# Splitting w1 of all experts once, into DRAM, in a float32 macaron kernel on one core

## The reference

```
x = x + 0.5 * ffn(layernorm(x))
x = x + attn(layernorm(x))
x = x + 0.5 * ffn(layernorm(x))
```

```
probs = softmax(mean(h, tokens) @ gate_w); top_w, top_i = top_k(probs, 2); top_w /= sum(top_w)
y_e = gelu(h @ w1[e] + b1[e]) @ w2[e] + b2[e];  out = sum over the two of top_w[e] * y_e
```

## Time and profile before

| what | value |
|---|---|
| median of three runs | 274.96 us |
| the profiled execution, its own time | 275.18 us |
| its span | 273.4 us |
| TensorE (PE) busy | 255.6 us (93%) |
| VectorE (DVE) busy | 222.6 us (81%) |
| ScalarE (ACT) busy | 207.2 us (76%) |
| GpSimd (POOL) busy | 45.6 us (17%) |
| granted TensorE clock, mean | 0.997 of full |
| read from HBM, written | 11.85 MB, 2.10 MB |

### The profile page before, as it was taken

How to read it: one execution, slowest core, us unless ns; L and a number is a source line. 1 busy time by engine, 2 the same in 40 slices (tenths; PEclk the granted TensorE clock), 3 DMA queues, 4 the chain that set the end, 5 groups by cost and what they waited for, 6 DMA issues and landing times.

```text
span 273.4 us, 3572 instructions
## 1 busy us (share of the span) xinstructions
PE 255.6 (93%) x1056; PEld 177.2 (65%) x1056; DVE 222.6 (81%) x567; ACT 207.2 (76%) x254; POOL 45.6 (17%) x58
## 2 busy tenths in 40 slices
PE   0899999999999989999999999997999999999994
PEld 0796676665656656666566566564777778778781
DVE  3569578559999999999999999999999997546252
ACT  1069584558998959969889979889996697689462
POOL 5320200430006002533006151003000030000000
PEclk9999999999999999999999999999999999999998
DMA  7364310022000022000400005000000500820005
GB/s 208 140 174 135 103 54 0 0 74 84 1 0 0 2 73 82 1 2 0 151 5 0 2 2 154 0 0 2 0 0 2 157 0 0 224 86 0 0 0 153
DMA packets 13762, 14.17 MB, mean 52 GB/s; under 512 B 1008, under 2 KB 9456, under 8 KB 13744
## 3 DMA queue, kind: packets, MB, share of 16 engines
q1 hardware_dynamic: 12720, 12.37, 15.3%
q0 software_dynamic: 352, 1.31, 1.2%
q10 hardware_dynamic: 672, 0.27, 0.4%
HBM read 11.85 MB, written 2.10 MB: 51 GB/s over the span
## 4 chain that ended last, share of the span: by engine, by line
PE 72%; ACT 8%; DVE 8%; issue 7%; DMA 3%; SPq 1%; POOL 0%; ACTq 0%; DVEq 0%; POOLq 0%
PE y_ps L684 32%; PE hid_ps L655 25%; PE aux_ps L752 3%; PE aux_ps L708 3%; PE aux_ps L784 3%; PE aux_ps L733 2%; PE aux_ps L773 2%; ACT vb L558 2%; PE y_ps L792 1%; DMA xt<-x_dram 1%; DVE hid_lo L931 1%; ACT dt_t L547 1%; DMA w_sb<-wpack_dram 1%; ACT hid L475 1%; ACT yt L504 1%
## 5 line engine op out<-in xcount | busy, mean ns | idle before, releaser
L475 ACT ACTIVATE hid<-hid_ps,w_sb 128x1024 f32<-128x1024 f32 x64 | 70.2, 1108 | 19.9 <-PE hid_ps L655 19.6
L684 PE MATMUL y_ps<-hid,w_sb 128*128 128x512 f32 x168 | 79.2, 594 | 0.0
L655 PE MATMUL hid_ps<-z_hi,w_hi 128*128 128x512 f32 x128 | 51.6, 484 | 0.8 <-ACT hid L475 0.8
L684 PEld LDWEIGHTS y_ps<-hid,w_sb 128*128 128x128 f32 x168 | 30.8, 190 | 22.9 <-issue 20.3
L931 DVE TENSOR_TENSOR hid_lo<-hid,hid_hi 128x1024 fp32r<-128x1024 f32 x22 | 26.6, 1222 | 19.8 <-ACT hid_hi L482 19.8
L655 PE MATMUL hid_ps<-z_lo,w_hi 128*128 128x512 f32 x128 | 39.9, 393 | 0.0
L655 PE MATMUL hid_ps<-z_hi,w_lo 128*128 128x512 f32 x128 | 39.8, 392 | 0.0
L655 PEld LDWEIGHTS hid_ps<-z_hi,w_hi 128*128 128x128 f32 x128 | 23.1, 189 | 16.1 <-issue 12.4
L655 PEld LDWEIGHTS hid_ps<-z_hi,w_lo 128*128 128x128 f32 x128 | 24.0, 188 | 5.5
L655 PEld LDWEIGHTS hid_ps<-z_lo,w_hi 128*128 128x128 f32 x128 | 24.0, 188 | 5.5
L482 ACT ACTIVATE hid_hi<-hid 128x1024 fp32r<-128x1024 f32 x22 | 22.7, 1055 | 1.5 <-PE y_ps L684 1.4
(11 more groups left out here) (119 smaller groups left out, 438.7 us busy)
## 6 DMA issues: line engine op xcount, KB each, us to landing
w_sb<-wpack_dram SPq DMA_DIRECT2D x16, 256.5 KB, 3.5
w_sb<-wpack_dram SPq DMA_DIRECT2D x15, 258.0 KB, 3.0
xt<-x_dram SPq DMA_DIRECT2D x3, 512.0 KB, 7.1
out_dram<-xt SPq DMA_DIRECT2D x3, 512.0 KB, 5.8
rope_sb<-rope_dram POOLq DMA_DIRECT2D x1, 1024.0 KB, 7.9
out_dram<-xt SPq DMA_DIRECT2D x2, 256.0 KB, 2.4
xt<-x_dram ACTq DMA_DIRECT2D x1, 256.0 KB, 4.0
xt<-x_dram SPq DMA_DIRECT2D x1, 256.0 KB, 3.6
```

The lines of the kernel that those rows point to most:

```text
L475: nc.scalar.activation(hid[:, slot % HBUF, :], hid_ps[:, slot % 2, :], ACT.Gelu, bias=bias).then_inc(hid_ready, 1)
L655: last = nc.tensor.matmul(hid_ps[:, slot % 2, cols], w, z[:, q % 2, cols], start=first, stop=end)
L684: last = nc.tensor.matmul(y_ps[:, cols], wt, src[:, cols], start=t == 0 and i == 0, stop=t == SLOTS - 1 and end)
```

## The change

What it does:

- w1 of all 8 experts is loaded once into SBUF (w1_all, 2 MB, in two transfers: the first 256 hidden units of every expert before x of batch 1, the rest behind the first expert loads). It uses the space of the mixer's state, gated, va and vb, which are written only when w1_all has been read. ScalarE and VectorE split each expert (c_pre_hi, c_pre_lo at places 206 to 550), four buffers shared with dt_t, decay, alpha and u; SyncE writes high and low parts to an internal DRAM tensor w1_split (8 times 512 KB).
- Passes 2 to 7 load w1's two parts from w1_split (512 KB per expert), ready for up; L465 and L884 are gone for them. Pass 0 splits its two experts' blocks from w1_all (the first two blocks) and from two transfers of its own; pass 1 splits from w1_all. Pass 2's load waits for all eight writes.
- b1 moves from the transfer of w1 to that of w2; a gelu at f = 0 now waits for w2_in[k].
- w2 of the first expert is left unscaled, that of the second is scaled by ratio = coef1 / coef0 (a reciprocal and a multiply on VectorE per pass), and pass_out scales y by coef0.
- The three small operations of mixer_carry_decay go to GpSimd (mixer_carry_steps, places 741, 1166, 1347, 1766). dstep's first value of each chunk is set once to -1000, so that its exponential is 0, in place of the memset of alpha in every mixer.
- The opening: x of batch 0 comes in four quarters; the tiles are turned first, copied out in two halves with their sums, and these sums give the logits; the ones products before the first tile are 13, those behind the logits 5. in_chunk is made earlier on GpSimd; rope is loaded by SyncE, behind x(3), instead of GpSimd.
- PARTS is 3, 0, 0, 0, 0, 3, 4, 4. All places are new. The up and gelu of slot s stand at 40 s + 40, a down at 40 s + 98 or, by parts, 40 s + 132, which is 40 later each. On TensorE m_dt stands at 649, 949, 1309, 1706 and m_v at 669, 989, 1349, 1746; on VectorE f_route at 309, 545, 937, 1258, 1504, 1847, 2189 for passes 1 to 7, m_cos first at 709.

The diff, cut to its core:

```diff
-DOWN = {False: 58, True: 92}
-
-PARTS = {0: 2, 1: 0, 2: 0, 3: 0, 4: 0, 5: 3, 6: 3, 7: 3}
+DOWN = {False: 98, True: 132}
+
+PARTS = {0: 3, 1: 0, 2: 0, 3: 0, 4: 0, 5: 3, 6: 4, 7: 4}
...
+        "f_norm": {1: 166, 2: 306, 3: 749, 4: 1089, 5: 1449, 6: 1806, 7: 2126},
+        "f_route": {1: 229, 2: 449, 3: 926, 4: 1249, 5: 1489, 6: 1829, 7: 2166},
...
+        "c_split_rest": {0: 75, 1: 201},
+        "c_proj": {0: 151},
+        "c_pre_lo": {0: 232, 1: 385, 2: 391, 3: 463, 4: 470, 5: 517, 6: 523, 7: 550},
+        "c_mixer": {0: 487},
+        "f_stats": {1: 81, 2: 207, 3: 400, 4: 959, 5: 1312, 6: 1712, 7: 2053},
...
+        "c_split_rest": {0: 19, 1: 130},
+        "c_pre_hi": {0: 206, 1: 226, 2: 233, 3: 384, 4: 392, 5: 450, 6: 460, 7: 500},
+        "c_proj_hi": {0: 220},
...
+        "m_rms": {0: 459, 1: 773, 2: 1113, 3: 1477},
+        "m_carry": {0: 741, 1: 1166, 2: 1347, 3: 1766},
...
+        "c_pre_out": {0: 238, 1: 392, 2: 397, 3: 472, 4: 479, 5: 525, 6: 532, 7: 560},
+        "f_load": {1: 315, 2: 567, 3: 939, 4: 1262, 5: 1510, 6: 1856, 7: 2195},
...
-    B1_AT, W2_AT, B2_AT = F, F + FT, 2 * F + FT
+    B1_AT, W2_AT, B2_AT = 0, FT, FT + F
+    PRE_BUF = 4
     HBUF = 4
-    WARM = 14
+    WARM_EARLY, WARM = 13, 5
+    HEADS = 2
...
+        late = sb("late", [P, 4, N])
+        state, gated, va, vb = (late[:, i, :] for i in range(4))
+        w1_all = late[:, :, :].rearrange("p a n -> p (a n)").rearrange("p (e n) -> p e n", e=E)
+        w_sb = sb("w_sb", [P, 2, TOP, PACK - F])
...
+        w1_parts = sb("w1_parts", [P, 2, TOP, 2, F], F32R)
+        w1_hi, w1_lo = w1_parts[:, :, :, 0, :], w1_parts[:, :, :, 1, :]
+        w1_split = nc.dram_tensor("w1_split", [E, P, 2 * F], F32, kind="Internal").ap()
...
-                src = []
                 for k in range(TOP):
                     e = sp.value_load(top_i[0:1, k:k + 1], min_val=0, max_val=E - 1)
-                    src.append(wpack[bass.ds(e, 1), :, :].rearrange("e p n -> p (e n)"))
-                    head = P if q == 0 and k == 0 else 0
-                    if head:
-                        sp.dma_start(w_sb[:, 0, 0, 0:head], src[k][:, 0:head]).then_inc(w1_head_in, 16)
-                    sp.dma_start(w_sb[:, q % 2, k, head:W2_AT], src[k][:, head:W2_AT]).then_inc(w1_in[q % 2][k], 16)
-                for k in range(TOP):
-                    sp.dma_start(w_sb[:, q % 2, k, W2_AT:], src[k][:, W2_AT:]).then_inc(w2_in[q % 2], 16)
+                    if q >= 2:
+                        if q == 2 and k == 0:
+                            for i in range(PRE_BUF):
+                                sp.wait_ge(pre_out[i], 16 * (E // PRE_BUF))
+                        sp.dma_start(w1_parts[:, q % 2, k, :, :].rearrange("p a n -> p (a n)").bitcast(F32),
+                                     w1_split[bass.ds(e, 1), :, :].rearrange("e p n -> p (e n)")).then_inc(w1_in[q % 2][k], 16)
+                    if q == 0:
+                        sp.dma_start(w1_first[:, k, :], wpack[bass.ds(e, 1), :, HEADS * P:F].rearrange("e p n -> p (e n)")
+                                     ).then_inc(w1_first_in[k], 16)
+                    sp.dma_start(w_sb[:, q % 2, k, :],
+                                 wpack[bass.ds(e, 1), :, F:].rearrange("e p n -> p (e n)")).then_inc(w2_in[q % 2][k], 16)
+
+            def keep_split(e):
+
+                sp.wait_ge(pre_hi, e + 1)
+                sp.wait_ge(pre_lo, e + 1)
+                sp.dma_start(w1_split[e], mix_tmp[:, e % PRE_BUF, :]).then_inc(pre_out[e % PRE_BUF], 16)
...
-            sp.dma_start(xt[:, 0, 0:NT // 2, :], x0[:, 0:NT // 2, :]).then_inc(x_in[0], 16)
+            for i in range(2):
+                sp.dma_start(xt[:, 0, 2 * i:2 * i + 2, :], x0[:, 2 * i:2 * i + 2, :]).then_inc(x0_in[i], 16)
             sp.dma_start(gate_sb[:, :], gate_w).then_inc(small_in, 16)
+            sp.dma_start(w1_all[:, :, 0:HEADS * P], wpack[:, :, 0:HEADS * P].rearrange("e p n -> p e n")).then_inc(w1_heads_in, 16)
             load_x(1)
             load_experts(0)
+            sp.dma_start(w1_all[:, :, HEADS * P:], wpack[:, :, HEADS * P:F].rearrange("e p n -> p e n")).then_inc(w1_tails_in, 16)
             load_x(2)
             load_x(3)
+            sp.dma_start(rope_sb[:, :, :], rope.rearrange("k p n -> p k n")).then_inc(rope_in, 16)
...
+            def mixer_carry_steps(b):
+
+                pool.wait_ge(cumd_done, b + 1)
+                if b:
+                    pool.wait_ge(small_exp, b)
+                nc.gpsimd.tensor_scalar(small[:, 0, :], first_of(decay), -1.0, None, ALU.mult).then_inc(first_done, 1)
+                nc.gpsimd.tensor_scalar(ncd[:, :], cumd[:, :], cumd[:, 0:1], DECAY_MAX,
+                                        ALU.subtract, ALU.min).then_inc(ncd_done, 1)
+                pool.wait_ge(ncd_done, b + 1)
+                nc.gpsimd.tensor_tensor(small[:, 1, 1:NCH], ncd[:, 0:NCH - 1], ncd[:, 1:NCH],
+                                        ALU.subtract).then_inc(small_done, 1)
...
+            chosen = []
+
+            def split_first():
+
+                act.wait_ge(w1_heads_in, 16)
+                act.wait_ge(index_ready, 1)
+                chosen.extend(act.value_load(top_i[0:1, k:k + 1], min_val=0, max_val=E - 1) for k in range(TOP))
+                for f in range(HEADS):
+                    rows = slice(f * P, (f + 1) * P)
+                    nc.scalar.activation(w1_hi[:, 0, 0, rows],
+                                         w1_all[:, bass.ds(chosen[0], 1), rows].rearrange("p e n -> p (e n)"),
+                                         ACT.Copy).then_inc(w1_head_hi, 1)
+            def split_rest(k):
+
+                if k:
+                    nc.scalar.activation(w1_hi[:, 0, k, 0:HEADS * P],
+                                         w1_all[:, bass.ds(chosen[k], 1), 0:HEADS * P].rearrange("p e n -> p (e n)"),
+                                         ACT.Copy).then_inc(w1_hi_ready, 1)
+                act.wait_ge(w1_first_in[k], 16)
+                nc.scalar.activation(w1_hi[:, 0, k, HEADS * P:], w1_first[:, k, :], ACT.Copy).then_inc(w1_hi_ready, 1)
+
+            def split_second(q):
+
+                act.wait_ge(w1_tails_in, 16)
+                act.wait_ge(index_ready, q + 1)
                 for k in range(TOP):
-                    head = P if q == 0 and k == 0 else 0
-                    if head:
-                        act.wait_ge(w1_head_in, 16)
-                        nc.scalar.activation(w1_hi[:, 0, 0, 0:head], w_sb[:, 0, 0, 0:head],
-                                             ACT.Copy).then_inc(w1_head_hi, 1)
-                    act.wait_ge(w1_in[q % 2][k], 16 * (q // 2 + 1))
-                    nc.scalar.activation(w1_hi[:, q % 2, k, head:], w_sb[:, q % 2, k, head:F],
+                    e = act.value_load(top_i[0:1, k:k + 1], min_val=0, max_val=E - 1)
+                    nc.scalar.activation(w1_hi[:, q, k, :], w1_all[:, bass.ds(e, 1), :].rearrange("p e n -> p (e n)"),
                                          ACT.Copy).then_inc(w1_hi_ready, 1)
+
+            def presplit_hi(e):
+
+                act.wait_ge(w1_tails_in, 16)
+                if e >= PRE_BUF:
+                    act.wait_ge(pre_out[e % PRE_BUF], 16 * (e // PRE_BUF))
+                nc.scalar.activation(mix_tmp[:, e % PRE_BUF, 0:F].bitcast(F32R), w1_all[:, e, :],
+                                     ACT.Copy).then_inc(pre_hi, 1)
...
+                if f == 0:
+                    act.wait_ge(w2_in[q % 2][k], 16 * (q // 2 + 1))
...
-                                         bias=bias2[:, q % 2, :]).then_inc(yt_ready, 1)
+                                         bias=bias2[:, q % 2, :], scale=coef[:, q % 2, 0:1]).then_inc(yt_ready, 1)
...
+            turn_z(0)
             read_logits(0)
-            turn_z(0)
+            split_first()
             top_tanh(0)
-            split_w1(0)
...
-                for slot in slot_at(tick, 0):
+                for slot in slot_at(tick, TICKS):
...
+            for _ in range(WARM_EARLY):
+                nc.tensor.matmul(hid_ps[:, 0, 0:P], ones[:, :], ones[:, :], start=True, stop=True)
+            pe.wait_ge(made_ident, 2)
+            pre_norm(0)
...
+            def presplit_lo(e):
+
+                dve.wait_ge(pre_hi, e + 1)
+                V.tensor_tensor(mix_tmp[:, e % PRE_BUF, F:].bitcast(F32R), w1_all[:, e, :],
+                                mix_tmp[:, e % PRE_BUF, 0:F], ALU.subtract).then_inc(pre_lo, 1)
...
+                V.reciprocal(inverse[:, :], coef[:, q % 2, 0:1]).then_inc(inverse_ready, 1)
+                dve.wait_ge(inverse_ready, q + 1)
+                V.tensor_tensor(ratio[:, q % 2, :], coef[:, q % 2, 1:2], inverse[:, :], ALU.mult).then_inc(ratio_ready, 1)
...
-                V.tensor_scalar(small[:, 0, :], first_of(decay), -1.0, None, ALU.mult).then_inc(first_done, 1)
+                    dve.wait_ge(small_done, b)
                 V.tensor_tensor_scan(cumd[:, :], last_of(decay), cum_cap[:, :], 0.0,
```

(8 more changed lines are left out.)

384 lines of the change are left out of this document (227 added, 157 removed), and 6 rows, old and new, of the table AT.

## The result

The changed kernel takes 268.97 us (median of 4 runs, 268.60 to 269.13) against 275.12 for the kernel before on the same chip: a ratio of 0.9777, 95% interval 0.9757 to 0.9798, so 6.1 us less. The forecast was 269.8. The profiled execution took 268.60 us with a span of 266.8, against 275.18 and 273.4: 6.6 us less span. The experiments ran beside runs of the kernel before whose median was 275.1 to 275.6, so they are compared by ratio; 0.001 is 0.28 us.

The account below looks back on a forecast made before the run. TensorE was taken to bound the kernel, with VectorE also full beside the mixers. Parts 2.0 less, last slot 0.5 more, waits 2.2 less and opening 1.5 less make 5.2 us less: 269.8 us, range 266.0 to 274.4.

Parts of the forecast that it names:

- Parts, 2.0 less: Passes 0, 6, 7: 28 instead of 22 slots by parts, each 1.40 instead of 1.72 us, 2.0 us less TensorE work.
- The last slot, 0.5 back: Tail: by parts, the last slot's first half is complete later, so yt overlaps less; 0.5 us more, between 0 and 0.86.
- Waits, 2.2 less: Middle stretch with the mixers: VectorE relieved by about 8 us, so TensorE's 5.15 us of waits shrink by 2.2.
- Rival 1: Middle stretch: VectorE's relief is worth nothing, the 5.15 us of waits are ScalarE's; 272.0 us, chance 0.16.
- Opening, 1.5 less: Opening: earlier index, first up and gelu; up 4 done at about 28.5 us, 1.5 us less, ends 0 and 3.4.
- last tile 9.97: Opening: the last normalised tile ends at 9.97 us, from which the index follows at about 12.95, 0.3 earlier.
- Transfers at nothing: Passes 2 to 7: the 512 KB loads of w1 parts, taken as 4.5 us, all fit their covers; cost nothing.
- Rival 4: Mixers: carry steps held on GpSimd make ScalarE wait 16 us, half reaching TensorE; 277.8 us, chance 0.09.

Follow-up runs that it names:

- the order by halves: The changed kernel with the last slot's six matmuls ordered half by half, all three terms of half 0, then of half 1: 269.25 us, ratio 0.9776.
- the last run: The changed kernel with 9 warming products behind the logits and slot 63, the very last, back in plain float32: 268.44 us, ratio 0.9748.

## Why the prediction was right, and where not

The forecast was 5.2 us less against the profiled execution, and its span is 6.6 less. That the median came within 0.8 us of the forecast is in part luck: the opening and the waits gave 2.4 us more than the sum had, the parts and the tail 1.0 less.

**Parts, 2.0 less: 1.2 measured** by TensorE's busy time, though six times 1.72 less 1.40 is work that it doesn't do; taken back, they are worth 2.3. The time of ScalarE and VectorE for it was costed at nothing because both had time to spare in those stretches. In the changed kernel that held: TensorE is idle 0.01 us from 20.20 to 66 us and 0.04 from 215 on. But the reason given doesn't carry it, since put alone into the kernel before, where there is as much to spare, the slots cost 6 us, most of it behind one hid_lo. Spare time of an engine over a stretch is not slack of each slot, nor of what stands behind it, and the prediction never priced that.

**The last slot, 0.5 back: 0.7 measured, the mechanism right.** The overlap of yt with the last matmuls fell from 0.74 to 0.11 us, which is the 0.6 that the prediction had before it took a little off for issue gaps; 0.1 more comes behind yt's start. The last hid_lo is just in time: the last two matmuls' weights wait 0.18 us for it, but the matmuls start 0.46 us behind the two before them (260.34 and 259.88), as those did. What it does is to keep the order by halves from helping, and the prediction didn't look at when it is there. That this slot should stay plain is shown by the last run.

**Waits, 2.2 less: 2.9 measured** by TensorE's idle time, 2.1 if the 0.8 us by which TensorE's busy time came out long is put here. The reason given was VectorE's relief. For the same work of TensorE in the mixers VectorE does some 7 us less (144.53 us beside 141.85 of TensorE before, 142.48 beside 146.80 now), where the sum had 8; an estimate. The runs with dummy work show that in the new order VectorE's load reaches the end at one half and ScalarE's at a fifth; that relief without the new places would have given the same is not shown. Rival 1 (worth nothing) would have left the 5.15 us of waits; 2.24 are left. VectorE was forecast under 140 us in 147; it is 142.48 in 149, 140.6 of 147: just missed. The sum took less than half of the waits because some were ScalarE's; over half went.

**Opening, 1.5 less: 3.2 measured, the one term well off.** The end of up 4 was put at 28.5 and came at 26.94. Of these 1.6 us, 1.0 is the index: predicted out at 12.95, out at 11.94. The step "last tile 9.97" kept the time of the earlier trace rows, but the last tile is done at 9.14. The first statistics begin at 3.35 in place of 4.37, x coming in quarters, and VectorE's last four tiles start at 8.02 and take 1.12 us in place of 8.45 and 1.52; beside the latter GpSimd filled in_chunk (0.95 us from 8.37), which the change makes earlier. Whether that is what stretched them was not tried. A further 0.2 is w2's transfer (gelu 1.2 earlier in all, at 16.21 where 17.4 was said), and 0.4 the walk from gelu 0 to the end of up 4, 11.1 us said and 10.73 measured. The upper end of this term, 3.4, had the result in it. The mechanism, first blocks without a transfer, is borne out by the run that undoes it: 3.2 us back, of which some 1.5 are the transfer. The rest of the gain is the earlier index (1.3 us) and a gelu that no longer stands behind the rounding of the second expert's w1.

**Transfers at nothing: right.** With another 512 KB in front of each the w1 parts still come in time, and w2 of pass 7 no longer does. The write to DRAM took 2.8 us where 5.8 had been taken.

**Rival 4: its mechanism came, its price did not.** The GpSimd steps were held in mixer 3, by 3.4 us together, but where ScalarE had other work: 0.7 us of waiting there, none on TensorE. The Trainium skill (SBUF — State Buffer, SBUF: two separate sides) says that a VectorE operation with two SBUF inputs holds the shared port pair for its whole length and a GpSimd operation that reads SBUF then blocks; the trace agrees, as each held step ends within 0.2 us of the end of such a tensor_tensor. That it costs little here is a matter of places, and the run with the steps on VectorE is slower.

## What to carry to other kernels

Before more work is given to an engine that has time to spare over a stretch, price the slack of one unit of it, from the instruction that makes its input to the one that waits for its output, and look at what stands behind it in that engine's order: a routing step behind an instruction that waits is late with all that hangs on it. Where a middle stretch is full on two engines, try how much of a dummy operation reaches the end, for each engine alone; that gives the exchange rate for edits that add such work to this order. Where a run undoes one thing, read in its chain of waits that the edit moved nothing else. And the last unit of a kernel is to be chosen for how early its first half is complete, not for its total cost.

## What the runs showed of the hardware

- Around the 1.45 us without work ahead of the first up, TensorE's granted clock falls to 0.50 for some 6 us in some executions of the same kernel and stays at 1.00 in others; with four more small products there it fell in none of 15 executions (mean 0.993 to 0.998). The Trainium skill (TensorE: Matmul & The Clock Gate, Part 1: The HAM clock gate) says that the half rate is the default and activity releases it, and that when it is released varies from run to run with the same kernel; here the fall does, at 0.984 and 0.996 mean clock of one kernel.
- 512 KB written to DRAM out of SBUF landed 2.8 us after issue (8 writes), 512 KB read from there 4.3 (12 reads); 128 KB asked for right behind the index landed after 2.0.
- ScalarE took 1.4 to 1.5 us to read two indexes out of SBUF into its registers: from 11.94 to 13.44 us in the changed kernel, from 14.91 to 16.30 in the run that fetches the first blocks.
- A small GpSimd step of 0.2 to 0.4 us takes up to 2.2 us beside VectorE operations with two inputs in SBUF, also where these are plain subtractions and products; in the earlier trace rows it was a scan.
